# A gated graph network: the residual in a buffer of its own, its bias added in eight pieces, and one block for both programs

## The reference, cut to what matters

```
Af = adj.astype(float32); state = x
for _ in range(5):
    a_in  = Af   @ (state @ in_W.T  + in_b)
    a_out = Af.T @ (state @ out_W.T + out_b)
    a = concat([a_in, a_out, state])
    r = sigmoid(a @ r_W.T + r_b)
    z = sigmoid(a @ z_W.T + z_b)
    h = tanh(concat([a_in, a_out, r * state]) @ h_W.T + h_b)
    state = (1 - z) * state + z * h
out = tanh(state @ o1_W.T + o1_b) @ o2_W.T + o2_b
return layernorm(x + out)
```

## Time and profile before

| | us |
|---|---|
| median of 3 runs | 714.21 (712.16 to 715.25) |
| the profiled execution, whole | 710.79 |
| its span, first to last instruction | 708.9 |
| PE busy in the span | 683.9 |
| DVE busy | 470.6 |
| ACT busy | 239.1 |
| POOL busy | 45.2 |

### The profile page before, as it was taken

One profiled execution on the slowest core, in us unless ns is written; L12 is line 12 of the kernel. 1 busy time (PEld: TensorE's weight loads), 2 busy tenths in 40 slices (PEclk: granted clock), 3 DMA queues, 4 the chain that ended last, 5 costly groups with the idle time before them and its releaser, 6 DMA issues.

```text
span 708.9 us, 8256 instructions
## 1 busy us (share of the span) xinstructions
PE 683.9 (96%) x3168; PEld 568.0 (80%) x3168; DVE 470.6 (66%) x775; ACT 239.1 (34%) x369; POOL 45.2 (6%) x38
## 2 busy tenths in 40 slices
PE   6999999999999999999999999999999999998991
PEld 6887888888888888888888888888888888886881
DVE  4777757876475767657676854657485565758794
ACT  2755645531132143203123511413252121214553
POOL 0022022000000000000000000000000000005052
PEclk9999999999999999999999999999999999999997
DMA  8873632000000000000000000000000000030003
GB/s 281 280 229 108 191 100 95 1 1 0 1 0 1 1 1 0 0 0 0 0 0 0 0 0 0 0 0 0 0 0 1 0 1 1 0 120 0 1 1 121
DMA packets 18414, 27.26 MB, mean 38 GB/s; under 512 B 1872, under 2 KB 9424, under 8 KB 18384
## 3 DMA queue, kind: packets, MB, share of 16 engines
q1 hardware_dynamic: 16864, 26.48, 11.3%
q10 hardware_dynamic: 1520, 0.40, 0.3%
HBM read 24.78 MB, written 2.10 MB: 38 GB/s over the span
## 4 chain that ended last, share of the span: by engine, by line
PE 87%; DVE 6%; DMA 3%; ACT 2%; issue 0%; SPq 0%; ACTq 0%; DVEq 0%
PE bank L432 37%; PE bank L375 15%; PE bank L377 15%; PE bank L376 15%; PE bank L404 2%; PE bank L515 2%; DVE a L805 2%; DMA stage<-in_adj_dram 1%; DMA stateT<-in_L_gnn_out_W_dram 1%; DVE rows L786 1%; ACT a L779 1%; DVE work L868 1%; DVE a L1087 1%; PE bank L384 0%; DVE ring L786 0%
## 5 line engine op out<-in xcount | busy, mean ns | idle before, releaser
L432 PE MATMUL bank<-ring,rows 128*128 128x512 f32 x1280 | 295.5, 390 | 0.9 <-ACT ring L600 0.7
L432 PEld LDWEIGHTS bank<-ring,rows 128*128 128x128 f32 x1280 | 239.5, 188 | 51.3 <-ACT ring L600 1.6
L634 ACT ACTIVATE work<-work,bias 128x512 f32<-128x512 f32 x120 | 86.6, 724 | 286.3 <-DVE work L862 285.7
L862 DVE SCALAR_TENSOR_TENSOR work<-degree,deg_w,bank 128x512 f32<-128x512 uint16 x120 | 88.9, 744 | 109.8 <-PE bank L377 109.4
L375 PE MATMUL bank<-u_c,fold 128*128 128x512 f32 x240 | 96.6, 402 | 3.1 <-DVE work L862 3.1
L791 DVE CAST ring<-a 128x1024 fp32r<-128x1024 uint8 x128 | 87.0, 688 | 12.7 <-PE bank L432 12.7
L377 PE MATMUL bank<-u_c,fold 128*128 128x512 f32 x240 | 93.8, 391 | 0.0
L376 PE MATMUL bank<-u_c,fold 128*128 128x512 f32 x240 | 93.7, 390 | 0.0
L377 PE MATMUL bank<-st_c,own 128*128 128x512 f32 x160 | 62.4, 390 | 0.0
L375 PE MATMUL bank<-st_c,own 128*128 128x512 f32 x160 | 62.3, 390 | 0.0
L376 PE MATMUL bank<-st_c,own 128*128 128x512 f32 x160 | 62.2, 389 | 0.0
(11 more groups left out here) (120 smaller groups left out, 733.3 us busy)
## 6 DMA issues: line engine op xcount, KB each, us to landing
stage<-in_adj_dram SPq DMA_DIRECT2D x28, 512.0 KB, 5.2
work<-in_x_dram SPq DMA_DIRECT2D x1, 2048.0 KB, 16.1
a<-in_x_dram SPq DMA_DIRECT2D x1, 2048.0 KB, 8.3
a<-in_adj_dram SPq DMA_DIRECT2D x3, 512.0 KB, 11.1
out_dram<-a SPq DMA_DIRECT2D x3, 512.0 KB, 3.0
a<-in_L_gnn_r_W_dram SPq DMA_DIRECT2D x1, 768.0 KB, 6.8
a<-in_L_gnn_z_W_dram SPq DMA_DIRECT2D x1, 768.0 KB, 8.8
stateT<-in_L_gnn_h_W_dram SPq DMA_DIRECT2D x1, 768.0 KB, 10.4
```

What stands on the lines that cost most here:

```text
L432: last = nc.tensor.matmul(u_bank[2 * (c % 2) + d][:, :], rows[:, part, j, d * P:(d + 1) * P], ring[:, p % RING, jj, :], start=(j == 0 and ...
L634: nc.scalar.activation(gates[:, g, e, :], gates[:, g, e, :], ACT.Tanh if g == H else ACT.Sigmoid, bias=bias[:, g, e:e + 1]).then_inc(gate_ ...
L862: nc.vector.scalar_tensor_tensor(out=gates[:, g, e, :], in0=degree[:, c * CW:(c + 1) * CW], scalar=deg_w[:, g, e:e + 1], in1=g_bank[s % 3] ...
```

## The change

1. The residual gets a buffer `res` of three chunks; its fourth chunk goes into `deg_sum`, which is free once the degrees are summed. The scratch output of the check, which lay in `deg_sum`, gets a buffer of its own.
2. SP loads the residual in four pieces right behind the last load of the matrix in step 0; the fourth waits until ACT has read the last degree sums.
3. POOL adds the bias in eight instructions of 128x512 elements. Piece b waits for `pair_ready` to reach 32 + 8(b + 1), so that four start in step 1 and four in step 2, each when DVE has expanded the last pair of a chunk.
4. There is one block for both programs, and no barrier between them. DVE signals `flag_ready` with the flag, and each engine loads and tests it when its own work of the fast program is done. SP loads the flag after its last store is issued, waits for the stores, and then tests; only if the flag isn't zero does it raise `fast_done`, for which the others then wait.

The diff, cut to its core (changed arguments and the same test on PE, ACT and DVE are left out):

```diff
+        res = sb("res", [P, NC - 1, BC * D])
+        scratch = sb("scratch", [P, CW], U8)
...
-        scratch = deg_sum[:, 0:CW // 4].bitcast(U8)
...
-        x_res = late.rearrange("p (b d) -> p b d", d=D)
+        x_res = [r.rearrange("p (b d) -> p b d", d=D) for r in [res[:, c, :] for c in range(NC - 1)] + [deg_sum[:, :].bitcast(F32)]]
...
-        block = ctx.enter_context(nc.Block())
...
-            sp.wait_ge(pair_ready, N_STEPS * S_PAIR)
-            sp.dma_start(x_res, x_v).then_inc(xr_loaded, 16)
-
-            starts = [c * BC for c in range(NC)] + [NB - BC // 2, NB]
+            for c in range(NC):
+                if c == NC - 1:
+
+                    sp.wait_ge(deg_part_ready, NC)
+                sp.dma_start(x_res[c], x_v[:, c * BC:(c + 1) * BC, :]).then_inc(xr_loaded, 16)
+
...
-            sp.wait_ge(y_stored, 16 * (len(starts) - 1))
...
-            pool.wait_ge(xr_loaded, 16)
-            for c in range(NC):
-                xr = x_res[:, c * BC:(c + 1) * BC, :]
-                nc.gpsimd.tensor_tensor(xr, xr, o2_bb[:, :].unsqueeze(1).broadcast_to([P, BC, D]), ALU.add)\
+            pool.wait_ge(xr_loaded, 16 * NC)
+            for b in range(NB // 2):
+                pool.wait_ge(pair_ready, S_PAIR + 8 * (b + 1))
+                xr = x_res[b // 2][:, b % 2 * 2:b % 2 * 2 + 2, :]
+                nc.gpsimd.tensor_tensor(xr, xr, o2_bb[:, :].unsqueeze(1).broadcast_to([P, 2, D]), ALU.add)\
                     .then_inc(residual_ready, 1)
...
-                nc.vector.tensor_copy(flag, t_bank[0:1, 0:1]).then_inc(odd_link, 1)
+                nc.vector.tensor_copy(flag, t_bank[0:1, 0:1]).then_inc(flag_ready, 1)
...
-                dve.wait_ge(residual_ready, c + 1)
+                dve.wait_ge(residual_ready, 2 * (c + 1))
...
-            with sp.If(sp.value_load(flag, min_val=0, max_val=MISMATCHES) != 0):
+            sp.wait_ge(flag_ready, 1)
+            found = sp.value_load(flag, min_val=0, max_val=MISMATCHES)
+            sp.wait_ge(fast_stored, 16 * fast_stores)
+            with sp.If(found != 0):
+
+                sp.sem_inc(fast_done, 1)
...
+            pool.wait_ge(flag_ready, 1)
             with pool.If(pool.value_load(flag, min_val=0, max_val=MISMATCHES) != 0):
+                pool.wait_ge(fast_done, 1)
...
-        fast_path(nc, flag[:, :], *args)
-        general_path(nc, flag[:, :], *args)
+          nc.semaphore("fast_stored") as fast_stored, nc.Block() as block):
+        fast_stores = fast_path(nc, block, flag[:, :], flag_ready, fast_stored, *args)
+        general_path(nc, block, flag[:, :], flag_ready, fast_stored, fast_stores, *args)
```

More of the change, by code:

```diff
@@ L39, in wait, with fast_path @@
         eng.wait_ge(sem, value)
-def fast_path(nc, flag, x, adj, in_W, in_b, out_W, out_b, r_W, r_b, z_W, z_b, h_W, h_b,
+def fast_path(nc, block, flag, flag_ready, y_stored, x, adj, in_W, in_b, out_W, out_b, r_W, r_b, z_W, z_b, h_W, h_b,
               o1_W, o1_b, o2_W, o2_b, out):
@@ L241, in fast_path @@
         std_ready = sem("f_std_ready")
-        y_stored = sem("f_y_stored")
         N_PREP = NG * 4 + 2
@@ L266, in fast_path @@
         BY_POOL = [2, 5, 9]
+        starts = [c * BC for c in range(NC)] + [NB - BC // 2, NB]
         TREE = [NB // 2 * CW // 4 >> n for n in range(4)]
-        block = ctx.enter_context(nc.Block())
         @block.sync
@@ L1087, in mean_and_variance @@
                     nc.vector.tensor_tensor(y[:, n:n + 2, :], out_bank[c][h][:, :].rearrange("p (b d) -> p b d", d=D),
-                                            x_res[:, n:n + 2, :], ALU.add).then_inc(o_read, 1)
+                                            x_res[c][:, 2 * h:2 * h + 2, :], ALU.add).then_inc(o_read, 1)
                 for n in range(c * BC, (c + 1) * BC):
@@ L1124, in _, with general_path @@
             normalize(BY_DVE[2])
-def general_path(nc, flag, x, adj, in_W, in_b, out_W, out_b, r_W, r_b, z_W, z_b, h_W, h_b,
+    return len(starts) - 1
+def general_path(nc, block, flag, flag_ready, fast_stored, fast_stores, x, adj, in_W, in_b, out_W, out_b, r_W, r_b, z_W, z_b, h_W, h_b,
                  o1_W, o1_b, o2_W, o2_b, out):
@@ L1179, in general_path @@
         bank = [pb(f"bank{i}", [P, CW]) for i in range(8)]
+        fast_done = sem("fast_done")
         loaded = sem("loaded")
@@ L1276, in _ @@
         def _(pe):
+            pe.wait_ge(flag_ready, 1)
             with pe.If(pe.value_load(flag, min_val=0, max_val=MISMATCHES) != 0):
+                pe.wait_ge(fast_done, 1)
                 pe.wait_ge(ident_ready, 1)
@@ L1382, in _ @@
         def _(act):
+            act.wait_ge(flag_ready, 1)
             with act.If(act.value_load(flag, min_val=0, max_val=MISMATCHES) != 0):
+                act.wait_ge(fast_done, 1)
                 with act.Fori(0, N_STEPS * NC) as q:
@@ L1401, in _ @@
         def _(dve):
+            dve.wait_ge(flag_ready, 1)
             with dve.If(dve.value_load(flag, min_val=0, max_val=MISMATCHES) != 0):
+                dve.wait_ge(fast_done, 1)
                 n = 0
@@ L1478, in gnn_kernel @@
 def gnn_kernel(nc, *args):
-    with nc.sbuf_tensor("flag", [1, 1], I32) as flag:
-        fast_path(nc, flag[:, :], *args)
-        general_path(nc, flag[:, :], *args)
+    with (nc.sbuf_tensor("flag", [1, 1], I32) as flag, nc.semaphore("flag_ready") as flag_ready,
+          nc.semaphore("fast_stored") as fast_stored, nc.Block() as block):
+        fast_stores = fast_path(nc, block, flag[:, :], flag_ready, fast_stored, *args)
+        general_path(nc, block, flag[:, :], flag_ready, fast_stored, fast_stores, *args)
 _INS = ["x", "adj"] + ["L0_gnn_" + n for n in ("in_W", "in_b", "out_W", "out_b", "r_W", "r_b", "z_W", "z_b", "h_W", "h_b",
```

## The result

| | before | after |
|---|---|---|
| median of 4 runs, us | 713.23 (712.16 to 715.25) | 703.72 (702.83 to 705.41) |
| ratio of the medians | | 0.987 (0.985 to 0.9889) |
| the profiled execution, us | 710.79 | 703.13 |
| its span | 708.9 | 701.3 |
| from the first gate of the last step's third chunk to the end | 72.35 | 64.27 |

The kernel is 9.5 us faster by the medians (7.9 to 10.7 by the interval), 7.7 us by the two profiled executions. 706.0 was predicted, with 702 to 710.5 as the range, and -8.2 us from the profiled execution. The forecast counted from the median of three runs, 714.21; with a fourth run the kernel before has 713.23.

The account below looks back on a forecast made before the run. PE was taken as the bound, so time is won only in its hole and behind its last matmul. -3.2, 0, 0 and -5.0 sum to -8.2 us, from 714.21 to 706.0; eight in ten within 702.0 to 710.5.

Parts of the forecast that it names:

- What bounds the kernel: Whole kernel: PE is busy 683.9 of 708.9 us; time is won only where PE stands still or behind its last matmul.
- the hole: PE idle at 646 to 649 us, waiting for DVE's late gate of line 862; said to cost 3.2 us.
- the end: After the last store, 703.5 to 708.8 us: barriers, flag loads and jumps with nothing else running; 5.0 us to win.
- Part 1: Last step, 640 to 660 us: without the late bias addition PE's wait closes, -3.2 us; bounds 0 and 3.2.
- Part 2: Steps 1 and 2: eight small additions hidden by DVE's idle time and lead, 0 us; outer bound 10.8.
- Rival (d): Steps 1 and 2: the eight additions take DVE's time in full from PE, +2.6 us, 716.8; chance 0.04.
- Part 3: Step 0: residual loads behind the matrix's last load cost 0 us, with 1.1 us of slack; kept bound 5.1.
- rival (c): Step 0: x loads delay the matrix's last load by their own length, 5.1 us; net -3.1, 711.1; chance 0.05.
- Part 4: Kernel's end: one block hides the jumps, the last store ends the kernel, -5.0 us; bounds 5.0 and 1.3.
- Rival (b): Kernel's end: PE's or DVE's fetch still ends last, up to 3.7 of 5.0 us lost; -4.5, 709.7; chance 0.11.
- The level: Whole kernel's median: 706.0 us, from a median of 714.21 less 8.2; uncertain by some 2 us either way.

Follow-up runs that it names:

- e11: New kernel with four bias additions of 128x1024 released when DVE has filled the first ring buffer for step 2, about 254 us; 707.86 us, ratio 0.9917.
- e3: New kernel with early loads kept, but four bias additions of 128x1024 at the first gate of the last step's third chunk; 706.74 us, ratio 0.9922.
- e1: New kernel with only the residual's part: own buffer, early loads, eight pieces; two blocks and the barrier between them as before; 707.90 us, ratio 0.9932.
- e9: New kernel with four bias additions of 128x1024 released when DVE has filled the last ring buffer of the last step; 703.45 us, ratio 0.9862.
- e4: New kernel without POOL's eight bias additions, the output bias left out of the result; 703.66 us, ratio 0.9859 to the kernel before.
- e6: New kernel with the eight additions in groups of three, three and two, released at the first ring buffer of steps 2, 3 and 4; 703.81 us, ratio 0.986.
- e8: New kernel without the second program: no flag load or test, SP only waits for the stores; 702.80 us, ratio 0.9856 to the kernel before.
- e2: New kernel with only the block's part: residual loaded late into the matrix's buffer, four late additions of 128x1024; 707.68 us, ratio 0.9938.
- e7: New kernel with the residual's loads held until DVE has filled three ring buffers for step 1; 703.57 us in one run.
- e10: New kernel with the eight additions of 128x512 released at the first gate of the last step's third chunk; 706.33 us, ratio 0.9903.
- e5: New kernel with POOL, PE, ACT and DVE also waiting for all stores before loading the flag; one block, one barrier; 707.80 us, ratio 0.9932.
- e12: Kernel before, unchanged, run and profiled once more; 711.40 us over 11 runs, ratio 0.9998.

## Why the prediction was right, step by step

**What bounds the kernel.** Held. Time came from the two places named, the hole and the end. In 120 to 640 us PE is busy 520.00 of 520.00 in every kernel of the table but e11 (515.81).

**Part 1, forecast -3.2.** Measured 3.4 ahead of ACT's last normalization, and taking the late additions away from e3 gives 3.3. DVE's chain to the owed gate is 4.3 us shorter (12.1 to 7.85), forecast 4.4. That POOL's additions beside DVE's chain make the hole is shown by e3 and e11, its price by e1 and e3. What the prediction didn't separate is the early load from the moved and halved additions: e9 shows that the load alone is enough.

**Part 2, forecast 0 with 10.8 as the bound.** 0: e4. The cover named was DVE's lead over PE in the ring, and it is real. DVE's casts take 89.0 us in all instead of 87.0, and wait 10.6 us for PE instead of 12.7: the 2 us come out of their waiting. Four of the eight pieces hold a DVE instruction, by 1.0 or 1.1 us each: a cast twice, and an instruction of the matrix check twice. One term was off without a consequence. I let POOL hold DVE for up to 1.35 us and put POOL's own instruction at 1.3; it took 1.57 to 2.27, since DVE's instructions hold POOL as well. Rival (d), that DVE would be one POOL instruction behind all the time, is refuted by e4, and even e6 found no such place for instructions of this size. With instructions of 128x1024 it exists (e11, 4.2 us).

The Trainium skill, "SBUF — State Buffer", section "The single rule", calls the ports that DVE and GpSimd share an exclusive lock: a DVE instruction with two inputs in SBUF contends with a GpSimd instruction that reads SBUF, and, as the section puts it for DVE's two-port modes, whichever issues first has the pair for its whole instruction and the other is blocked. By this rule, the trace agrees in both directions (DVE 2.88 us against 0.69, POOL 2.27 against 1.30 in the earlier trace rows), and e6's instruction with one operand in PE's bank wasn't held (0.69).

**Part 3, forecast 0, with 5.1 as the kept bound.** 0 in the time, but not because nothing happened: the last load of the matrix takes 0.9 us longer than before (4.3 against 3.4), and the slack of 1.1 us is down to 0.2. Its ring buffer is done at 119.36, not by 119 as I had written. A little more in that queue, and rival (c) would have begun.

**Part 4, forecast -5.0.** Measured 4.7. The missing 0.3 go with the stores, as e8, without jumps beside them, is 0.3 faster: the three 512 KB pieces land 3.5 us after their issue instead of 3.0, and the last two, of 256 KB, 3.6 instead of 3.1. In all runs with the jumps' fetches beside the stores the page says 3.5 (after, e2, e3, e4, e6, e7, e9, e10, e11), in those without 3.0 (before, e1, e5, e8, e12). In e5 SP still loads the flag beside its stores, so that load isn't what slows them; the other engines' flag loads and their jumps no run separates. DVE's fetch was longer too, and used up the margin of 0.15 us that I had given it: 4.2 or 4.3 us in eight kernels with this end (after, e3, e4, e6, e7, e9, e10, e11), where SP's drain stands 0.1 to 0.2 us behind DVE's. But in e2, beside the same stores, it took 3.7, and SP's drain came 0.8 behind it. Behind the stores it took 3.0 (before, e1, e12) and in e5 3.6. So some 0.6 us of DVE's fetch varies from kernel to kernel with the stores out of it, and how much of the 1.2 is theirs stays open. Rival (b) came true in its mechanism and not in its price: DVE's fetch is late by as much as it could be for nothing.

The Trainium skill, "Runtime: NRT & Kernel Launch", section "Instruction fetch mechanics", gives the fetch a DMA queue of its own. I had taken that for a sign that fetch and stores would leave each other alone; the measurement says that the stores land later beside the jumps (3.5 us against 3.0), and it decides. What the two share, no run here tells.

**The level, forecast 706.0.** 703.72, which is inside the range but 2.3 under the forecast. 1.0 of that is the median from which I counted (714.21, now 713.23). The part that the trace explains is 8.1 us, the medians say 9.5 (7.9 to 10.7), and e4, e6 and e9, all like the new kernel, lie 10.2, 10.1 and 9.4 us under the kernel before beside them. So the medians fell by 1 to 2 us more than the profiles, and what does it is open. That the trace's 8.1 meets the forecast 8.2 so closely is in part luck: part 1 came out 0.2 above, part 4 0.3 below. The profiled execution of before was faster than all four of the other runs (710.79 against 712.16 and up), and the medians of the kernel before themselves move from one set to the next: 713.87 beside e4 and e6, 711.96 and 711.40 in e12. Against these last two the new kernel's 703.72 would be 8.2 and 7.7 less, as the trace has it.

In the runs of the kernel before that stand beside the experiments the time goes with the mean granted clock: the eleven at 0.987 or less took 712.4 to 716.7 us, the six at 0.993 or more 710.7 to 712.3. A fall of the clock behind the hole, which cost 1.6 us in e10's profile, would be one source. But it was seen in one execution of a kernel that has a hole at this place, in the profiles of before, e2, e3, e11 and e12 the clock stayed at 1.00 behind holes of 2.8 to 3.2 us, and kernels without a hole have such runs too (e8: 705.09 at 0.991, its four others 702.66 to 702.87 at 0.995 to 0.997; e1: 709.47 at 0.988). So a lower clock in some runs is shown, and its tie to the hole is not.

No kernel here beats the new one clearly: e8 is 0.3 us faster by the trace but has no second program, and e7 and e9 are equal.

## What to carry to other kernels

When VectorE instructions with two operands in SBUF are slow for a few microseconds, look for GpSimd instructions beside them, and ask first what those waited for: here a transfer of 8.3 us had moved harmless work out of VectorE's idle time into the chain, and loading earlier cures that without touching the work. If they must overlap, the length of one GpSimd instruction sets the price of one wait (up to 1.1 us behind 128x512, 2.2 behind 128x1024), and the length of all of them sets how many waits there are. And a branch that every engine must take at the end belongs in front of the wait for the last stores, where it cost 0.3 us here instead of some 4.

## What the runs showed of the hardware that I had not expected

- Stores of 512 KB land 3.5 us after their issue beside the engines' flag loads and jumps (nine kernels), and 3.0 without them (five). DVE's own fetch took 3.0 us behind the stores (before, e1, e12) or 3.6 (e5: branch at 702.6, drain at 706.2), and 3.7 (e2) or 4.2 to 4.3 (eight kernels) beside them.
- Loading one word of SBUF into a register takes SP 0.89 to 0.99 us while it has stores in flight, and 0.47 once they have landed (before, e1, e12). DVE takes 0.54 to 0.62.
- The granted clock fell to 0.50 for about 3.4 us behind a hole of only 2.2 us (e10), at the end of hundreds of microseconds without one; behind holes of 2.8 to 3.2 us in five other profiles it didn't.
- Eight GpSimd instructions of half size were no cure by themselves. In e10 they took 12.3 us in all (8.91 + 3.40) against 10.82 for the four, so they reached further into DVE's chain, and the hole only went from 3.0 to 2.2 us.
